# Expert weights fetched in two parts on the queue of the bounce, flags kept in registers, token rows turned first in a tile

## The reference

```python
g = jnp.einsum('nd,efd->enf', xf, W_gate)
u = jnp.einsum('nd,efd->enf', xf, W_up)
y = jnp.einsum('enf,edf->end', jax.nn.silu(g) * u, W_down)
out = jnp.zeros_like(xf)
for k in range(TOP_K):
    out = out + y[top_idx[:, k], n_ar] * pi[:, k:k + 1]
```

## Time and profile before

| | |
|---|---|
| median of 3 runs | 2142.2 us (2135.87 to 2144.44) |
| profiled execution | 2141.04 us, span 2139.2 us |
| busy share of the span | PE 89%, ACT 65%, DVE 62%, POOL 33% |
| the stage of the experts | from 713 to about 1424 us of the span |
| PE in 721.3 to 1424.2 us | 642.61 us busy of 702.90 |

### The profile page before, as it was taken

The page is one execution under the profiler, slowest core; times in us unless marked ns, Lnnn a source line. Parts: engine busy times, 40 slices in busy tenths (PEclk is TensorE's granted clock), DMA queues, the critical chain, the costliest instruction groups (busy, mean ns, idle before and its releaser), DMA issues.

```text
span 2139.2 us, 37738 instructions
## 1 busy us (share of the span) xinstructions
PE 1907.4 (89%) x11671; PEld 1082.2 (51%) x11671; DVE 1330.8 (62%) x2221; ACT 1386.3 (65%) x1586; POOL 706.6 (33%) x696
## 2 busy tenths in 40 slices
PE   6999999999946599988998999968899999999998
PEld 5822333333332488877887778856622222222255
DVE  4611145446567656555565455437699999999967
ACT  5699999999933223233233233226699999999934
POOL 2000111111110212122222122111078888988922
PEclk9999999999955699999999999988999999999999
DMA  5744334444110654553554554549945435364012
GB/s 195 248 98 70 55 74 81 90 90 86 34 41 8 244 197 144 194 191 134 197 173 155 196 185 140 184 168 318 299 68 115 86 50 122 60 149 66 11 80 70
DMA packets 156033, 276.10 MB, mean 129 GB/s; under 512 B 18588, under 2 KB 99742, under 8 KB 155000
## 3 DMA queue, kind: packets, MB, share of 16 engines
q1 hardware_dynamic: 119960, 225.57, 38.7%
q10 hardware_dynamic: 29040, 29.23, 4.3%
q0 software_dynamic: 6816, 18.62, 2.6%
HBM read 365.58 MB, written 96.21 MB: 216 GB/s over the span
## 4 chain that ended last, share of the span: by engine, by line
PE 47%; ACT 22%; DVE 13%; DMA 7%; issue 7%; POOL 2%; DVEq 1%; ACTq 1%; SPq 0%; POOLq 0%
PE psum L2664 17%; PE psum L1345 12%; PE psum L1326 9%; ACT A1f_probs L1370 9%; ACT A1f_probs L1378 8%; DMA hidden<-e_squares 3%; PE psum L381 3%; DVE e_w_low L2585 2%; ACT e_w_high L2455 2%; DMA e_turned<-hidden 2%; PE psum L850 1%; DMA qk_parts<-L_part 1%; DVEq L2352 1%; DVE e_hT L2568 1%; PE psum L396 1%
## 5 line engine op out<-in xcount | busy, mean ns | idle before, releaser
L1326 PE MATMUL psum<-A_qa,A_ka 50*128 50x512 f32 x2048 | 408.0, 466 | 23.1 <-DVE A_qa L1413 6.2
L1326 PEld LDWEIGHTS psum<-A_qa,A_ka 50*128 50x128 f32 x2048 | 176.5, 185 | 471.9 <-DVE A1f_probs L1423 243.4
L2664 PE MATMUL psum<-e_w_high,e_xT 128*128 x1136 | 387.7, 404 | 20.6 <-DVE e_xT L2558 20.3
L1547 POOL TENSOR_TENSOR A1f_probs<-A1f_probs,A1f_bias 128x512 f32<-128x512 f32 x256 | 327.5, 1291 | 81.2 <-ACT A1f_probs L1378 80.9
L1423 DVE SCALAR_TENSOR_TENSOR A1f_probs<-psum,A1f_bias 128x1024 f32<-128x1024 f32 x256 | 311.6, 1217 | 23.6 <-PE psum L1326 20.3
L1378 ACT ACTIVATE A0f_probs<-psum 128x1024 f32<-128x1024 f32 x256 | 316.4, 1236 | 0.0
L1366 ACT ACTIVATE A0f_probs<-psum 128x1024 f32<-128x1024 f32 x256 | 314.0, 1227 | 3.0 <-PE psum L1326 2.9
L1345 PE MATMUL psum<-A1f_probs,v 128*32 128x512 f32 x2048 | 273.9, 606 | 17.6 <-POOL A1f_probs L1547 16.1
L1370 ACT ACTIVATE A1f_probs<-A1f_probs 128x1024 f32<-128x1024 f32 x256 | 273.9, 1070 | 4.6 <-DVE A1f_probs L1423 3.7
L1345 PE MATMUL psum<-A0f_probs,v 128*32 128x512 f32 x2048 | 274.0, 608 | 0.0
L2664 PE MATMUL psum<-e_w_high,e_hT 128*128 x1120 | 228.1, 296 | 41.4 <-DVE e_hT L2568 40.8
(11 more groups left out here) (302 smaller groups left out, 2541.5 us busy)
## 6 DMA issues: line engine op xcount, KB each, us to landing
e_w_raw<-in_experts ACTq DMA_DIRECT2D x69, 3072.0 KB
hidden<-e_squares SPq DMA_DIRECT2D x69, 512.0 KB
e_turned<-hidden SPq DMA_DIRECT2D x276, 128.0 KB
qk_parts<-L_part SPq DMA_DIRECT2D x64, 512.0 KB, 4.2
A_qa<-qk_parts SPq DMA_DIRECT2D x192, 128.0 KB, 4.3
A_ka<-qk_parts SPq DMA_DIRECT2D x192, 128.0 KB, 6.5
om<-results SPq DMA_DIRECT2D x16, 512.0 KB, 7.4
A1f_bias<-tables SPq DMA_DIRECT2D x16, 384.0 KB, 8.7
```

The costliest lines, as they stand in the source:

```text
L1326: mm = e.matmul(ps[:, side * HALF:(side + 1) * HALF], self.qk.ka[rows, s, pair, kt * P:(kt + 1) * P].bitcast(FP32R), self.qk.qa[rows, s, p ...
L1547: e.tensor_tensor(fourth, fourth, self.bias_of(*w[1:], slice(self.FOURTH, GH)).rearrange("p h q -> p (h q)"), ALU.mult).then_inc(self.mult ...
L2664: mm = e.matmul(out, left[part].bitcast(FP32R), moving.bitcast(FP32R), start=start and i == 0, stop=stop and i == 2)
```

## The change

Conditional fetches move from ACT to SP and are cut in two: for a new tile k, the gate and up words are fetched in SP's round k + 1 and the down words in round k + 2, each after the four loads of the bounce and before the next store. SP must first see that the high and low copies of that part are made. The third and fourth expert are fetched there too, in rounds 0 to 3. The longest run of bytes in one descriptor grows from 1024 to 4096. The flags that an engine uses several times are kept in registers: on ACT and DVE the second and third test of `IS_NEW` reads no table. DVE splits the token rows before it makes the low "up" part, and PE turns the token rows of tile j + 1 as the first thing of tile j. The early load of the next stage's rows (`beside(e, (2, 3))`, 1024 KB) moves from before SP's loop to its round 8.

```diff
-WEIGHT_RUN = 1024
+WEIGHT_RUN = 4096
...
+    def flag(self, e, flags, row, j):
+        if (row, j) not in flags:
+            flags[row, j] = self.planned(e, row, j)
+        return flags[row, j]
...
+    def fetch_next(self, e, flags, j, part, sem):
+        a, b = part
+        e.dma_start(self.w.raw[:, bass.ds(self.flag(e, flags, OTHER_BUFFER, j), 1), a:b],
+                    self.w.weights[bass.ds(self.flag(e, flags, FOURTH, j), 1), :, a:b].rearrange("e p n -> p e n"),
+                    cond=self.flag(e, flags, IS_NEW, j) > 0, max_dma_last_dim=WEIGHT_RUN).then_inc(sem, DMA)
...
     def sync(self, e, mirror_stored, beside):
         e.wait_ge(self.rows_in[1], DMA)
         mirror_stored(e)
-        self.fetch(e, 0, SECOND, 0, self.second_in)
+        self.fetch(e, 0, SECOND, (0, WIDE), self.second_in)
         e.wait_ge(self.first_low, 3)
-        beside(e, (2, 3))
+        flags = {}
         for j in range(self.BY_PE):
             self.store_squares(e, j)
             self.load_turned(e, j)
+            self.fetch_parts(e, flags, j)
+            if j == 8:
+                beside(e, (2, 3))
...
+    def fetch_parts(self, e, flags, j):
+
+        up, down = (0, DOWN_AT), (DOWN_AT, WIDE)
+        if j == 0:
+            self.fetch(e, 1, THIRD, up, self.weights_in)
+        elif j == 1:
+            e.wait_ge(self.high_ready, self.high_value("second", self.REST))
+            self.fetch(e, 1, THIRD, down, self.second_in)
...
+        if 2 <= j < 2 + self.LAST_FETCH:
+            e.wait_ge(self.high_ready, self.high_value("up", j))
+            e.wait_ge(self.low_ready, self.low_value("up", j - 1))
+            self.fetch_next(e, flags, j - 1, up, self.weights_in)
+        if 3 <= j < 3 + self.LAST_FETCH:
+            e.wait_ge(self.high_ready, self.high_value("down", j - 1))
+            e.wait_ge(self.low_ready, self.low_value("down", j - 2))
+            self.fetch_next(e, flags, j - 2, down, self.second_in)
...
-        def high_part(j, a, b):
-            with e.If(self.planned(e, IS_NEW, j) > 0):
-                e.wait_ge(self.weights_in, DMA * min(max(1, j - 1), MOE_TILES - 1 - self.LAG))
+        def high_part(j, kind, a, b):
+            with e.If(self.flag(e, flags, IS_NEW, j) > 0):
+                n = min(max(0, j - 2), self.LAST_FETCH)
+                if kind == "down":
+                    e.wait_ge(self.second_in, DMA * (2 + n))
+                else:
+                    e.wait_ge(self.weights_in, DMA * (1 + n))
...
-            if self.LAG < j < self.LAST:
-                fetch_fourth(j - self.LAG)
...
+            if j + 1 < MOE_TILES:
+                split_rows(j + 1)
             if j > 1:
                 low_part(j - 1, "up", DC * F, DOWN_AT)
-            if j + 1 < MOE_TILES:
-                split_rows(j + 1)
...
         for j in range(MOE_TILES):
+            if j + 1 < MOE_TILES:
+                turn_rows(j + 1)
             if j >= 1:
                 wait_for_weights(j)
             up_product(j, 0)
-            if j + 1 < MOE_TILES:
-                turn_rows(j + 1)
```

More of the change, by code:

```diff
@@ L2318 @@
     LAST = MOE_TILES - 1
+    LAST_FETCH = LAST - 3
     Q, R = 4, 32
@@ L2399, in sync @@
             self.load_turned(e, j)
-        e.wait_ge(self.second_in, DMA)
-        e.wait_ge(self.weights_in, DMA * (MOE_TILES - 1 - self.LAG))
+            self.fetch_parts(e, flags, j)
+            if j == 8:
+                beside(e, (2, 3))
+        self.fetch_parts(e, flags, self.BY_PE)
+        e.wait_ge(self.second_in, DMA * (2 + self.LAST_FETCH))
+        e.wait_ge(self.fourth_in, DMA * 2)
+        e.wait_ge(self.weights_in, DMA * (1 + self.LAST_FETCH))
         e.wait_ge(self.downed, self.BY_PE + 1)
         beside(e, (0, 1))
+    def fetch_parts(self, e, flags, j):
[5 more added lines that the diff above has]
+            self.fetch(e, 1, THIRD, down, self.second_in)
+        elif j == 2:
+            e.wait_ge(self.low_ready, self.low_value("second", self.REST))
+            self.fetch(e, 0, FOURTH, up, self.fourth_in)
+        elif j == 3:
+            e.wait_ge(self.high_ready, self.high_value("up", j))
+            self.fetch(e, 0, FOURTH, down, self.fourth_in)
+        if 2 <= j < 2 + self.LAST_FETCH:
+            e.wait_ge(self.high_ready, self.high_value("up", j))
+            e.wait_ge(self.low_ready, self.low_value("up", j - 1))
[4 more added lines that the diff above has]
+            self.fetch_next(e, flags, j - 2, down, self.second_in)
     def store_squares(self, e, j):
@@ L2461, in high_second @@
             e.drain().then_inc(self.high_ready, 1)
-        def high_part(j, a, b):
-            with e.If(self.planned(e, IS_NEW, j) > 0):
-                e.wait_ge(self.weights_in, DMA * min(max(1, j - 1), MOE_TILES - 1 - self.LAG))
+        def high_part(j, kind, a, b):
[5 more added lines that the diff above has]
+                    e.wait_ge(self.weights_in, DMA * (1 + n))
                 if j >= 2:
-                    e.wait_ge(self.fourth_in, DMA)
+                    e.wait_ge(self.fourth_in, DMA * (2 if kind == "down" or j > 3 else 1))
                 high_of(bass.ds(self.planned(e, OTHER_BUFFER, j), 1), a, b)
             e.drain().then_inc(self.high_ready, 1)
[L2471 to L2475, removed]
         def move_y(j):
@@ L2503, in act @@
             e.activation(self.hid[:, :], self.GU[:, 0, :], ACT.Silu).then_inc(self.silu, 1)
[L2504 to L2509, removed]
-            if self.LAG < j < self.LAST:
-                fetch_fourth(j - self.LAG)
             if 1 <= j < self.LAST:
                 e.wait_ge(self.upped, j)
-                high_part(j, 0, DOWN_AT)
+                high_part(j, "up", 0, DOWN_AT)
             if j == self.LAST:
@@ L2518, in act @@
                 move_y(j - self.LAG)
-                high_part(j - 1, DOWN_AT, WIDE)
+                high_part(j - 1, "down", DOWN_AT, WIDE)
             if j + 1 == self.REST:
```

10 lines of the change are left out of this document (6 added, 4 removed).

## The result

The changed kernel is slower: a median of 2160.45 us in 6 runs (2152.66 to 2164.91) against 2142.99 for the kernel before (6 runs, 2135.87 to 2144.44). The ratio is 1.0085 with an interval of [1.0062, 1.0107]. The prediction said 2101 us, range 2092 to 2122, and gave "slower" 6 in 100. It was wrong in sign.

The account below looks back on a forecast made before the run. The stage of the experts was taken as bound by PE, with a hundred microseconds of stops to win. From 2141.0, gains of 33.9 + 0 + 1 + 6.6 = 41.5 gave 2099.5; with the median 1.2 higher, 2101 us, range 2092 to 2122.

Parts of the forecast that it names:

- Work hidden: SP's rounds: about 2.6 us more per round fits between last load and next store, so it costs nothing.
- Kind (b): Seven long rounds three tiles after a change of expert, where fetch and bounce collide; nearly gone, 33.9 us gained, bounds 20 and 36.
- the up part takes over 6 us: Sign at the fetch of the gate and up words: if moving them takes over 6 us, the prediction is wrong.
- U: Time origin: PE's first gate product two tiles after the new one; loads must have landed by U + 20.2.
- B: Rival: one queue's strict order holds the bounce 2 us beyond the limit at seven changes; gain 17.5, 2125 us; chance 0.25.
- E: Rival: slower, as the up part moves at less than half the rate; 2186 us at a third; chance 0.06.
- Change of expert: Rounds at the seven changes of expert: 0 us in all, bounds 14 us gain and 6 us loss.
- Start: Gap at the stage's start: second expert's fetch goes alone, so PE starts earlier; 6.6 us gained, bounds 4 and 9.
- The moved rows: The next stage's early load of rows, moved to SP's round 8, was said to have slack there.

Follow-up runs that it names:

- the kernel with hoisted reads: The changed kernel with SP's three table reads per round moved from behind the bounce's loads to between store and loads: 2128.59 us, ratio 0.9923 to the kernel before.
- the kernel with the fetch where ACT is idle: The changed kernel with the two conditional fetches on ACT's queue, after the high copy of the up part: 2125.62 us, ratio 0.9905 to the kernel before.

## Why the prediction was wrong

**"Work hidden … SP gets about 2.6 us more per round … nothing": this step failed.** The 2.6 us was nearly right (2.17 + 0.66 measured). What was wrong is the test: I asked whether the work fits between the last load and the next store of an undisturbed round, and it does. I did not ask how much slack the chain keeps. Store, landing, loads, reads and fetches are one chain of 7.30 us on one queue, so a bounce that is held is 1.3 us less late one round later, not 4.2. Taking the three reads out of the chain gave 31.9 us, and adding three cost 85. This step turned a standstill into a loss; it is not the whole of the miss, since the kernel with hoisted reads is still 27.5 us above the 2101 that were forecast.

**Kind (b), 33.9 us gained: this step failed too, in the hold of the two stores behind a part.** The sum gave the up part 1.2 us to start and 5.1 to 5.6 to move; it had moved 8.0 us after its issue, 2.10 MB in about 7 us behind a start of 1.1, some 300 GB/s where the sum took 376 to 410 (7.8 to 8.8 us over the seven changes). It gave the down part 2.6 to 2.8 us to move; it was through 5.2 us after its issue. So "the up part takes over 6 us", one of the signs that the prediction named, came true. Placed on its scale, with U at 859.96: the bounce one tile earlier was stored at U + 0.7 (said: 0.7), the up part was issued at U + 7.5 (said: 7.2), and the loads behind it at U + 18.0 (said: 16.1, bound 2 late), 10.5 us after the fetch where the sum had 8.9. Then SP still had loads, reads and a fetch to issue. By the prediction's own numbers (16.1 + 1.73 + 2.1 + a fetch of 1) the next store could not leave before about U + 21, while two rounds after the first it was due at U + 17.9. It left at U + 23.2, was held 6.81 us, and PE stopped until 897.29. The stops of kind (b) were kept: 100.00 us for seven rounds in place of 96.08, and 48.5 us too much in the 28 rounds behind the changes in place of 36.3. With the reads hoisted it is 35.8: the hold alone, the loads issued 11.9 us after the fetch at the first change and 9.2 us for the store behind the down part, uses up the whole gain. Why the part moves more slowly here than the stage's first 3072 KB stays open.

**Rivals.** B had half of this mechanism: a hold longer than the sum allows. But it priced a stop at 3.7 us where the long rounds have 5.7 too much each, and it had no price for the rounds between. E had the sign; the up part was slower than summed, but by a fifth to a quarter of the rate and not by half, and the sign of the result needed the reads.

**Change of expert, 0 us, bounds +14 and -6.** ACT does wait for SP's count, 27.6 us in seven waits, but on PE the fourteen rounds at the changes sum to 159.14 us against 156.20 before, 2.9 us lost. The number lies within the bounds, and that is luck. Registers and order bring these rounds from 35.9 to 30.9 us too much (10 us in all, for which my sum had next to nothing), and the fetches on SP take 8.0 back, more than the 6 of the late bound: at the first change the copy starts 6.3 us after SiLU where 4 were said.

**Start, 6.6 us, bounds 4 and 9.** From the stage's first transposition to the first down product behind the gap are 30.1 us (722.23 to 752.34) in place of 34.5 (718.93 to 753.46): 4.4 us. The mechanism was right. The row of PE's timeline:

```profile
752.34 0.58 PE L2696 MATMUL psum<-e_w_high,e_hT 128*128 x1 [6.36 <-DVE e_hT L2599]
```

Behind the wait stands DVE's low copy of 6.56 us, which now starts at 744.29 (745.42 before) in a stage that begins 3.3 us later. The next rounds, 10.17, 10.13 and 9.52 us, give 4.0 us of it back, for which the sum had no term.

**The moved rows "have slack in round 8".** In the changed kernel they have not: at 830.60 the round is 14.35 us, 5.8 too long. The store behind them leaves only 4.2 us into its round and its loads come 7.18 us later:

```profile
824.52 1.66 SPq L319 DMA_DIRECT2D L_x<-x  x2
826.29 0.37 SPq L2451 DMA_DIRECT2D hidden<-e_squares  x1
833.47 1.74 SPq L2461 DMA_DIRECT2D e_turned<-hidden  x4
```

With the reads hoisted the rows stand in the same place, the store leaves as its round begins and takes 3.79 us, and the round is 8.55. So this was the length of the chain once more, and the slack was there without the reads.

**The sum as measured,** for the 19.6 us by which the stage grew: 3.9 (the seven long rounds) + 8.3 (the other 21 rounds behind the changes, twelve of them 8.8 to 9.8 us long, where the bounce is late and catches up slowly) + 2.9 (the changes) + 5.7 (moved rows) - 0.4 (start) - 0.9 (all others).

What stays open: how much of the 31.9 us comes through the late bounce and how much through the late count, since the hoisted reads cure both and each can act in the rounds at a change and behind it; and what slows the two parts of the fetch.

## What to carry to other kernels

Before work is put on a queue that "has time", add up its chain from one issue to the next with everything that waits in order (landing, loads, reads, issues), and subtract it from the round: what is left is how fast a delay is made good, and it matters more than whether the work fits. Put reads of a table where the queue waits for a landing anyway. Issue a large fetch right behind a small urgent transfer and not just ahead of one; in this kernel another queue alone did not protect it. And when two kernels do their work in another order, compare stretches that hold the same work.

## What the runs showed of the hardware

A store on its own queue that is issued just behind a large fetch of another queue starts late. Of the kernel with the fetch where ACT is idle, all DMA queues in 853.8 to 857.5 us (packets, MB, share), with the store issued at 853.82 on q1 and the fetch at 852.65 on q10, and then these two in 858.0 to 861.5:

```profile
q10 hardware_dynamic: 273, 1.12, 95.9%
```

```profile
q10 hardware_dynamic: 166, 0.67, 49.7%
q1 hardware_dynamic: 129, 0.50, 34.5%
```

For 3.7 us after its issue no packet of the store moved; then the two queues shared the engines. The Trainium skill, page "DMA: Bandwidth & Descriptors", section "Queues, rings and completion order", says that each DMA engine goes round-robin between the queues that have work. The second of the two answers agrees. The first shows no sharing; whether the store's work already stood in its queue then, the trace does not show, so the rule alone does not give the time. What was measured is 8.41 us beside a fetch, against 7.93 and 9.61 behind one in the same queue.

One table value read into a register costs SP 0.56 us (2.17 - 0.50 over three), and six cost the same each. The Trainium skill, page "DMA: Bandwidth & Descriptors", section "Latency and other measured facts", gives a floor of about 600 ns for such a load; the trace is just under it. Two conditional fetches that move nothing cost SP 0.66 us, and ACT, which waited for their count, went on 0.74 us after their issue began.
